# 16-wide cross attentions: scores in 64 and 33 rows with heads in pairs, the row of maxima by one copy and one transfer

## The reference, cut to what matters

```python
def cross(query, key, value, Wq, bq, Wk, bk, Wv, bv, Wo, bo):      # query = layernorm(x), key = value = ctx
    q = (query @ Wq.T + bq).reshape(b, -1, 16, 16)                 # 16 heads, 16 wide
    k = (key @ Wk.T + bk).reshape(b, -1, 16, 16)
    v = (value @ Wv.T + bv).reshape(b, -1, 16, 16)
    attn = softmax(einsum('bqhd,bkhd->bhqk', q, k) / 4)            # 256 queries, 4096 keys
    return einsum('bhqk,bkhd->bqhd', attn, v).reshape(b, -1, 256) @ Wo.T + bo
x = x + cross(...)
```

## Time and profile before

| what | value |
|---|---|
| median of three runs | 3472.56 us (3472.45 to 3473.24) |
| span of the profiled execution | 3477.2 us; the profile gives no other time for it, so it lies 4.6 us (0.13%) above the median |
| TensorE matmuls busy | 3203.5 us, 92% of the span |
| TensorE weight loads | 2079.1 us, 60% |
| VectorE busy | 2147.2 us, 62% |
| ScalarE busy | 1804.3 us, 52% |
| GpSimd busy | 846.7 us, 24% |
| granted TensorE clock, mean | 0.971 |
| first stage of the change, scores from | 2190.86 us to about 2536 us |
| second stage, scores from | 2842.86 us to about 3187 us |

### The profile page before, as it was taken

One profiled execution on the slowest core, in us unless ns is written; L12 is line 12 of the kernel. 1 busy time (PEld: TensorE's weight loads), 2 busy tenths in 40 slices (PEclk: granted clock), 3 DMA queues, 4 the chain that ended last, 5 costly groups with the idle time before them and its releaser, 6 DMA issues. The chain is left out here.

```text
span 3477.2 us, 55952 instructions
## 1 busy us (share of the span) xinstructions
PE 3203.5 (92%) x21616; PEld 2079.1 (60%) x21616; DVE 2147.2 (62%) x3342; ACT 1804.3 (52%) x2609; POOL 846.7 (24%) x654
## 2 busy tenths in 40 slices
PE   8989998999999999999769799999988889999689
PEld 6855695666666666666436676444455644445575
DVE  4336214666666666666488404999854289995764
ACT  4436211666666666667356231576745137676741
POOL 1042001344444444445147113000020030000440
PEclk9999999999999999999889899999999999999899
DMA  6259462000010000000586345865300396660110
GB/s 214 97 198 303 183 265 90 10 1 10 1 46 22 1 10 10 1 1 1 137 313 239 133 158 161 175 124 115 65 27 25 121 248 122 125 119 26 49 77 13
DMA packets 231636, 351.01 MB, mean 101 GB/s; under 512 B 104384, under 2 KB 177792, under 8 KB 226256
## 3 DMA queue, kind: packets, MB, share of 16 engines
q1 hardware_dynamic: 230992, 346.38, 34.0%
q0 software_dynamic: 384, 1.05, 0.1%
HBM read 261.35 MB, written 86.05 MB: 100 GB/s over the span
## 5 line engine op out<-in xcount | busy, mean ns | idle before, releaser
L1816 DVE TENSOR_REDUCE L1x_pk<-L1x_psm 128x2 f32<-128x1024 f32 x236 | 289.3, 1226 | 302.7 <-PE L1x_psm L1578 302.7
L1517 POOL TENSOR_TENSOR L1x_acc<-L1x_acc,L1x_pr 128x512 f32<-128x512 f32 x256 | 354.0, 1383 | 376.4 <-ACT L1x_pr L1749 358.3
L1749 ACT ACTIVATE L1x_pr<-L1x_pss 128x1024 f32<-128x1024 f32 x272 | 263.8, 1021 | 154.1 <-PE L1x_pss L1595 154.1
L1248 ACT ACTIVATE L2x_pr<-L2x_pss 128x1024 f32<-128x1024 f32 x256 | 248.1, 1021 | 104.2 <-PE L2x_pss L1143 103.9
L1248 ACT ACTIVATE L3x_pr<-L3x_pss 128x1024 f32<-128x1024 f32 x256 | 248.2, 1021 | 103.1 <-PE L3x_pss L1143 102.9
L1846 DVE TENSOR_TENSOR L1x_acc<-L1x_acc,L1x_pr 128x512 f32<-128x512 f32 x256 | 276.1, 1078 | 32.0 <-ACT L1x_pr L1749 19.5
L1271 DVE TENSOR_REDUCE L2x_pk<-L2x_psm 128x1 f32<-128x512 f32 x448 | 287.8, 686 | 12.1 <-PE L2x_psm L1100 8.4
L1271 DVE TENSOR_REDUCE L3x_pk<-L3x_psm 128x1 f32<-128x512 f32 x448 | 287.7, 686 | 11.2 <-PE L3x_psm L1100 7.6
L1739 ACT COPY L1x_pss<-L1x_neg 128x1024 f32<-128x1024 f32 x272 | 273.0, 1028 | 1.3 <-DVE L1x_pk L1816 1.3
L1608 PE MATMUL L1x_pso<-L1x_pr,L1x_V 128*64 128x256 f32 x2176 | 253.2, 383 | 0.6 <-DVE L1x_OT L1855 0.6
L1554 PE MATMUL L1x_psm<-L1x_cT,L1x_w 128*128 128x512 f32 x512 | 247.8, 607 | 1.6 <-DVE L1x_pk L1816 0.9
(11 more groups left out here) (766 smaller groups left out, 5852.6 us busy)
## 6 DMA issues: line engine op xcount, KB each, us to landing
f0e_wt<-in_f_pieces SPq DMA_DIRECT2D x10, 3072.0 KB, 10.7
offset_rows<-s_rows SPq DMA_DIRECT2D x32, 768.0 KB, 6.0
L2x_KS<-L2x_key_parts SPq DMA_DIRECT2D x24, 1024.0 KB, 12.9
L3x_KS<-L3x_key_parts SPq DMA_DIRECT2D x24, 1024.0 KB, 12.8
s_add<-offset_rows SPq DMA_DIRECT2D x32, 512.0 KB, 7.3
n_cT<-in_ctxT SPq DMA_DIRECT2D x32, 512.0 KB, 4.7
f1e_wt<-in_f_pieces SPq DMA_DIRECT2D x8, 2048.0 KB, 13.2
L2x_key_parts<-n_kst SPq DMA_DIRECT2D x32, 384.0 KB, 2.8
```

The source lines that it names most:

```text
L1248: nc.scalar.activation(pr[:, a % RING, :, :].rearrange("p h q -> p (h q)"), pss[:, 2 * (a % 2):2 * (a % 2) + 2, :].rearrange("p x q -> p ( ...
L1517: i = nc.gpsimd.tensor_tensor(acc[:, n, 1, :, :], acc[:, n, 1, :, :], pr[:, a % RING, :, 1, :], ALU.add)
L1749: nc.scalar.activation(pr[:, a % RING, :, :, :].rearrange("p h e q -> p (h e q)"), pss[:, x:x + 2, :].rearrange("p h n -> p (h n)"), ACT.E ...
L1816: nc.vector.reduce_max(pk[:, m, qt, :, j], peak_banks(z, qt), AX).then_inc(peak_read, 1)
```

## The change

The 97 rows of a score are cut into 64 (four pairs of parts, start of the sum) and 33 (two pairs of parts and the row of maxima, end of the sum). Heads go in pairs: the first two of a group lie in partitions 0 to 63 of `QS` and `KS`, the other two in 64 to 127, and the two matmuls of a pair use the two halves of the array and write different banks. So 4 matmuls per step become 8. The order of the heads in `pk`, `mx` and `pr` follows. The row of maxima is made by 2 matmuls with 4 output rows in one bank, one copy into `lows` (4x256) and one transfer on SP's queue into partitions 32 and 96 of `QS`; scores of a unit wait for it (`row_here`). `ROW_SLOT` is 26, and row and copy come behind the slot's products, averages and reads instead of ahead of its products and reads. Key stacks go in six transfers of half the size, query stacks in twelve, the ones in four memsets. ScalarE's loop is written with two indices and does the same. `ROOM` is the number of semaphores set aside.

```diff
-    ROW_SLOT = 28
+    ROW_SLOT = 26
-    ONE = len(KPART) * hd
+    ONE = 2 * hd
-        QS = u.sb(pre + "_QS", [P, NH, T], BF16)
+        QS = u.sb(pre + "_QS", [P, 2, NH // 2, T], BF16)
-        KS = u.sb(pre + "_KS", [P, 2, UH, CTX], BF16)
+        KS = u.sb(pre + "_KS", [P, 2, 2, 2, CTX], BF16)
+        lows = u.sb(pre + "_lows", [UH, 2, S], BF16)
...
             def stack(n, which=range(3)):
...
-                    parts = (of_half[:, 0:2], of_half[:, 0:2], of_half[:, 0:3:2])[x]
-                    sp.dma_start(into[2 * hd * x:2 * hd * (x + 1)], parts).then_inc(ks_in[n % 2], 16)
+                    for a in range(2):
+                        parts = (of_half[a][:, 0:2], of_half[a][:, 0:2], of_half[a][:, 0:3:2])[x]
+                        at = 64 * a + (0, 2 * hd, 0)[x]
+                        sp.dma_start(KS[at:at + 2 * hd, n % 2, x // 2, :, :].rearrange("p g n -> p (g n)"), parts).then_inc(ks_in[n % 2], 16)
+
+            def row(n):
+                b = n // NU
+                sp.wait_ge(turn_read, turns_with_row(n))
+                sp.dma_start(QS[ONE:64 + ONE + 1:64, 1, n % NU * 2:n % NU * 2 + 2, b * S:(b + 1) * S], lows[:, n % 2, :]).then_inc(row_here, 16)
...
             values(0)
+            row(0)
             stack(1)
             values(1)
             for n in range(UNITS - 2):
                 sp.wait_ge(peak, n + 1)
                 leading(n + 2)
+                row(n + 1)
                 sp.wait_ge(scored, STEPS * (n + 1))
                 stack(n + 2)
                 sp.wait_ge(averaged, STEPS * (n + 1))
                 values(n + 2)
+            row(UNITS - 1)
...
             def rows(n):
                 pe.wait_ge(peak, n + 1)
-                for e in range(2):
-                    x = claim()
-                    for h in range(2):
-                        for qt in range(QT):
-                            hq = (2 * e + h) * QT + qt
-                            i = nc.tensor.matmul(psm[ONE:ONE + 1, x % 3, h * S + qt * P:h * S + (qt + 1) * P], mx[:, n % 2, hq:hq + 1],
-                                                 k.less[:, :], start=True, stop=True)
-                    i.then_inc(turn, 1)
-                rows_out[n] = taken[0]
+                x = claim()
+                for qt in range(QT):
+                    i = nc.tensor.matmul(psm[0:UH, x % 3, qt * P:(qt + 1) * P], mx[:, n % 2, qt::QT], k.less[:, :], start=True, stop=True)
+                i.then_inc(turn, 1)
...
                 if s == 0:
-                    pe.wait_ge(turn_read, rows_out[n])
-                    pe.wait_ge(ks_in[n % 2], 16 * 3 * (n // 2 + 1))
+                    pe.wait_ge(row_here, 16 * (n + 1))
+                    pe.wait_ge(ks_in[n % 2], 16 * 6 * (n // 2 + 1))
...
-                for h in range(UH):
-                    i = nc.tensor.matmul(pss[:, 2 * (a % 2) + h // 2, h % 2 * S:(h % 2 + 1) * S], KS[0:ONE + 1, n % 2, h, s * P:(s + 1) * P],
-                                         QS[0:ONE + 1, n % NU * UH + h, b * S:(b + 1) * S], start=True, stop=True)
+                for g in range(2):
+                    for z, rows_of in enumerate((64, ONE + 1)):
+                        for h in range(2):
+                            at = slice(64 * h, 64 * h + rows_of)
+                            i = nc.tensor.matmul(pss[:, 2 * (a % 2) + h, g * S:(g + 1) * S], KS[at, n % 2, z, g, s * P:(s + 1) * P],
+                                                 QS[at, z, n % NU * 2 + g, b * S:(b + 1) * S], start=(z == 0), stop=(z == 1), skip_group_check=True)
                 i.then_inc(scored, 1)
...
-                    if x == ROW_SLOT and n + 1 < UNITS:
-                        rows(n + 1)
                     products(*of_slot(n, x))
                     if x % 2 == 0 and x >= 2:
                         average(n, x - 2)
                         average(n, x - 1)
...
+                    if x == ROW_SLOT and n + 1 < UNITS:
+                        rows(n + 1)
...
             def take_rows(n):
-                b, h0 = n // NU, n % NU * UH
-                for e in range(2):
-                    x = written()
-                    if n == 0:
-                        dve.wait_ge(qs_in, 16 * len(QPART))
-                    nc.vector.tensor_copy(QS[ONE:ONE + 1, h0 + 2 * e:h0 + 2 * e + 2, b * S:(b + 1) * S],
-                                          psm[ONE:ONE + 1, x % 3, :].rearrange("p (h q) -> p h q", h=2)).then_inc(turn_read, 1)
+                x = written()
+                if n >= 2:
+                    dve.wait_ge(row_here, 16 * (n - 1))
+                nc.vector.tensor_copy(lows[:, n % 2, :], psm[0:UH, x % 3, 0:S]).then_inc(turn_read, 1)
...
+                    read_peaks(*of_slot(n, x))
                     if x == ROW_SLOT and n + 1 < UNITS:
                         take_rows(n + 1)
-                    read_peaks(*of_slot(n, x))
```

More of the change, by code:

```diff
@@ L31 @@
 NH = 16
-ROOM = 40
+ROOM = 44
 NUMBERS = {}
@@ L978, in peak_of, with column, turns_with_row @@
             return i // (2 * 2 * QT), i // 4 % QT, i // 2 % 2 + 2 * (i % 2)
+        def column(h, qt):
+            return 4 * (h % 2) + 2 * (h // 2) + qt
+        def turns_with_row(n):
+            if n == 0:
+                return LATE + 1
+            return n + 1 + min(AHEAD + (NP // SLOTS) * (SLOTS * (n - 1) + ROW_SLOT + 1), NP * (UNITS - 1))
         def wide_banks(x):
@@ L1028, in _ @@
             for s, part in enumerate(QPART):
-                sp.dma_start(QS[s // 2 * 2 * hd + s % 2:(s // 2 + 1) * 2 * hd:2, :, :].rearrange("p (x h) s -> p x h s", h=UH), qscratch[part].rearrange("c (x r h) s -> r (c x) h s", r=hd, h=UH)).then_inc(qs_in, 16)
+                for a in range(2):
+                    at = 64 * a + s // 2 % 2 * 2 * hd + s % 2
+                    sp.dma_start(QS[at:at + 2 * hd - 1:2, s // 4, :, :].rearrange("p (x g) s -> p x (g s)", g=2),
+                                 qscratch[part].rearrange("c (x r a g) s -> a r (c x) (g s)", r=hd, g=2, a=2)[a]).then_inc(qs_in, 16)
             for j in range(NCH):
@@ L1055, in _ @@
             pool.wait_ge(sel_in, 1)
-            nc.gpsimd.memset(KS[ONE:ONE + 1, 0, :, :], 1.0).then_inc(ones_rows, 1)
-            pool.wait_ge(ones_rows, 1)
-            nc.gpsimd.memset(KS[ONE:ONE + 1, 1, :, :], 1.0).then_inc(ones_rows, 1)
+            for x in range(2):
+                for a in range(2):
+                    nc.gpsimd.memset(KS[64 * a + ONE:64 * a + ONE + 1, x, 1, :, :], 1.0).then_inc(ones_rows, 1)
+                    pool.wait_ge(ones_rows, 2 * x + a + 1)
         @block.tensor
@@ L1062, in _ @@
             taken = [0]
-            rows_out = {}
             def claim():
@@ L1154, in average @@
                 for h in range(UH):
[L1155 removed]
+                    i = nc.tensor.matmul(pso[32 * h:32 * h + VW, 0:S], V[:, n % 2, s, h * VW:(h + 1) * VW], pr[:, a % RING, 2 * (h % 2) + h // 2, :],
                                          start=(s == 0), stop=(s == STEPS - 1), skip_group_check=True)
@@ L1243, in _ @@
                                pss[:, 2 + n % 2, :].rearrange("p (t h e) -> p t h e", t=2, h=NH)).then_inc(v_ev, 1)
-            for a in range(UNITS * STEPS):
-                act.wait_ge(scored, a + 1)
-                if a >= RING:
-                    act.wait_ge(averaged, a - RING + 1)
-                nc.scalar.activation(pr[:, a % RING, :, :].rearrange("p h q -> p (h q)"),
-                                     pss[:, 2 * (a % 2):2 * (a % 2) + 2, :].rearrange("p x q -> p (x q)"), ACT.Exp, scale=SCALE).then_inc(exps, 1)
+            for n in range(UNITS):
+                for x in range(SLOTS):
+                    a = n * STEPS + x
+                    act.wait_ge(scored, a + 1)
+                    if a >= RING:
+                        act.wait_ge(averaged, a - RING + 1)
+                    nc.scalar.activation(pr[:, a % RING, :, :].rearrange("p h q -> p (h q)"),
+                                         pss[:, 2 * (a % 2):2 * (a % 2) + 2, :].rearrange("p x q -> p (x q)"), ACT.Exp, scale=SCALE).then_inc(exps, 1)
         @block.vector
@@ L1270, in read_peaks @@
                     x = written()
-                    nc.vector.reduce_max(pk[:, n % 2, h * QT + qt, j:j + 1], psm[:, x % 3, :], AX).then_inc(turn_read, 1)
+                    nc.vector.reduce_max(pk[:, n % 2, column(h, qt), j:j + 1], psm[:, x % 3, :], AX).then_inc(turn_read, 1)
                     if i == NP - 1:
@@ L1278, in read_first_peaks @@
                 dve.wait_ge(wide, x + 1)
-                nc.vector.reduce_max(pk[:, 0, h * QT + qt::2 * QT, j], wide_banks(x), AX).then_inc(wide_read, 1)
+                nc.vector.reduce_max(pk[:, 0, column(h, qt):column(h, qt) + 3:2, j], wide_banks(x), AX).then_inc(wide_read, 1)
                 if x == NP // 2 - 1:
```

16 lines of the change are left out of this document (7 added, 9 removed).

## The result

The changed kernel takes 3493.98 us (median of 4 runs, 3493.03 to 3499.45), the kernel before 3472.51 in the same comparison (3470.24 to 3473.24): 1.0060 times as long, with a 95% interval of 1.0048 to 1.0073. It is 21.5 us slower where 5.0 us faster was forecast, and lies above the range. The profiled execution has a span of 3491.2 us against 3477.2, so it shows 14.0 of the 21.5. These two make the other 7.5.

The account below looks back on a forecast made before the run. TensorE's instruction stream was taken to set the loop's period, VectorE's turn only 0.055 us behind. Pairs 11.0 and boundaries 6.7 saved, start 11.7 and denominators 1.0 lost: 5.0 us faster, 3467.5, range 3456 to 3488.

Parts of the forecast that it names:

- the two stops of before: TensorE stops in the old loops with nothing to wait for, 1.67 and 2.44 us, while keys and values load.
- rival 1: TensorE runs dry of instructions at each load: 12 stops of 3 us instead of 2, 30 us more, 3497; chance 0.14.
- Instruction supply: Delivery of TensorE's instructions in the unit loops, 128 more matmuls per unit; the main forecast gave it no added cost.
- The first row: Start of each stage: first maxima row lands with the values, scores begin 6.0 and 5.7 us late, 11.7 lost.
- Pairs: Pairs of slots in the unit loops: no shape switch around scores, 0.05 us saved each, 11.0 us in two stages.
- the turn without slack: Two products banks read by VectorE in turn, 1.25 us at best; faster TensorE would have to wait for it.
- Boundaries: Making the row of maxima between units: cheaper matmuls and copy, 0.6 us saved each, 6.7 us in two stages.
- The P behind the row: The next products matmuls where the maxima row is made: expected after 2.06 us instead of 1.31.
- Denominators: Seven per stage in the last unit, now differing in shape from scores: 0.1 us each, 1.0 lost in two stages.
- rival 2: Score matmuls on two array halves take 0.14 us a round instead of 0.11: 3486 us; chance 0.06.
- rival 3: Pairs of slots gain nothing, the turn already being 1.305 us; boundary savings stay, the start is lost: 3478.5; chance 0.10.
- S to P: Time from the start of scores to the next products on TensorE in the loop: 0.98 us before, 0.87 forecast.

Follow-up runs that it names:

- e5_cut_columns: Kernel before with the new row, its first transfer ahead of the values, each score matmul cut into two of 128 columns; loads bunched: 3511.1 us, ratio 1.0112.
- e14_before_paced: Kernel before with one edit, its loads spread over the units in twenty pieces each: 3468.7 us, ratio 0.9988.
- e13_97_rows_paced: Kernel before (97-row scores) with the new row, its first transfer ahead of the values, and loads spread in twenty pieces a unit: 3454.5 us, ratio 0.9943.
- e1_row_first: Changed kernel with the first row's transfer issued ahead of the first unit's values: 3484.5 us, ratio 1.0038.
- e12_fine_paced: Changed kernel with the first row's transfer ahead of the values and all loop loads spread in twenty pieces a unit: 3460.2 us, ratio 0.9950.

## Why the prediction was wrong

The step that failed is the supply of instructions: the forecast kept the two stops of before and gave more of them a cost of nothing, and put rival 1 at 0.14. Rival 1 held. Its mechanism was right and so was its count of twelve stops, but three of them had been there before, not two, and a stop costs 2.2 us with its slow clock (20.8 and 5.7 us over twelve, see the loads spread over the unit), not 3: 20.5 us instead of 30. That its total (3497 against 3494.0) looks closer than that is luck: 4.0 us less gain in the rest of the sum and 2 that are not explained make up for 6 of the 9.5.

- **Instruction supply**, forecast 0, rival 1 +30. With spread loads the loops of the changed kernel are 11.9 us shorter than those of before (666.1 and 678.0); with bunched loads they are 8.6 longer (695.1 and 686.6). So 20.5 us come from the bunched loads. By the step-by-step comparison above, 15.6 of them are the stops themselves (20.8 less 5.2), 4.2 the half clock behind some of them (5.7 less 1.5), and 0.7 the rest. The idle time in the table holds only 10.6. The argument that went wrong was "shorter key transfers may let instructions pass sooner". Each transfer was shorter, but all six were issued at once, as the three had been. The stops of the earlier trace rows were the warning, and the loads beside them the right suspect; 980 more matmuls per loop deserved more than one chance in seven. The Trainium skill ("Runtime: NRT & Kernel Launch", Instruction fetch mechanics) says that blocks of 256 instructions are fetched while the current one runs, mostly hidden. The blocks and their size agree with the trace: 2048 instructions more between the two 97-row kernels (x3504 and x4528 matmuls, and as many weight loads) and eight blocks more. "Mostly hidden" holds here where the loads are spread or absent; beside bunched loads a late block cost up to 3.4 us of idle time (e5_cut_columns).
- **The first row**, forecast +11.7, measured +10.9 from the starts and 9.5 from moving it. Right, and it was not the landing alone that came late: SP needed 3.55 us to issue the row behind the values.
- **Pairs**, forecast -11.0. The pair takes 2.57 (forecast 2.565) against 2.61. Between the two kernels with spread loads a unit falls from 42.68 to 42.11, and the loops by 3.5; with the denominators added back that is 6.6 us. A pair saves 0.04 instead of 0.05, and the turn without slack waits once more in each unit (13 waits of TensorE for reads in a loop against 7, 5.4 us against 4.1).
- **Boundaries**, forecast -6.7, measured -8.3 as the loops of e14_before_paced less those of e13_97_rows_paced. The P behind the row comes after 2.04 us (forecast 2.06).
- **Denominators**, forecast +1.0, measured +3.0: the last unit takes 36.74 us from first to last scores instead of 35.22, in every kernel with the new scores. In the timeline of the last unit they start 1.09 us after the scores where it was 0.88:

```profile
2502.59 1.16 PE L1164 MATMUL L2x_pss<-L2x_QS,L2x_KS 64*128 64x256 bf16 x16
2503.68 0.70 PE L1148 MATMUL L2x_psm<-L2x_OT,L2x_sel 128*128 128x256 f32 x2
```

  0.21 seven times is 1.5 a stage: twice the 0.1 of a change of shape that I had read from other pairs of instructions.
- **Halves side by side** (rival 2) and **no gain in the pairs** (rival 3) fell: S to P is 1.04 with VectorE's turn as the limit, where eight rounds of 0.14 alone would be 1.12, and the pair is shorter. **The later rows** were never waited for, as forecast.

Without the added stops the sum would have been -6.6 -8.3 +3.0 +10.9, that is 1.0 us faster than before: not the 5.0 of the forecast, but inside its own range. With the 20.5 of the stops it is 19.5 slower, as the loops and starts of the profile say (8.6 + 10.9). The last 2 of the measured 21.5 us lie outside both and are not explained.

## What to carry to other kernels

Count the instructions that an edit adds on the busiest engine, and look whether the profile already has stops marked "issue" beside heavy loads: if it has, more instructions can multiply them, and here each cost 2.2 us with the clock behind it. Where such stops all end at the same place in groups of 256 of the engine's instructions, it is the supply. The cure is cheap, independent of the edit, and took the stops away in all three kernels here that had them: issue the loads of the next block of work in small pieces over the whole of the current one, instead of all at once. And a small transfer on which the next matmul waits belongs ahead of the large ones in its queue.

## What the hardware showed that I had not expected

- A loop whose DMA share averages 0.51 starves TensorE of instructions because the loads are bunched, and the same bytes spread out do not (15.5 us of stops against 0). The DMA share itself falls with the spreading, from 0.54 at 109 GB/s to 0.46 at 114 and 113 (the windows of e1_row_first and e12_fine_paced).
- Fewer bytes can make it worse: without the values 27.3 us of stops instead of 15.7.
- All twelve stops of the changed kernel's loops end at the same place in groups of 256 TensorE instructions, 2.6 to 3.1 us after the transfer of a block began.
- A stop can be there or not with a small change of the program: the new row alone, 44 matmuls fewer a loop, took those of before away.
- The clock doesn't follow the length of a stop alone: it fell to half behind three of the twelve stops after (2.75, 2.68 and 2.26 us idle, for 3.4, 6.8 and 3.4 us), and before behind the one of 1.67 us but not behind the one of 2.44.
- The issue of a 2 KB transfer held SP for 3.55 us when a transfer of 1088 KB in packets under 512 bytes had been issued just ahead of it, and for 0.6 to 0.8 when it went first. In e1_row_first the key transfers behind the values took the delay instead: 6.98 us for the six of them, against 3.76.
